# Second attention layer: three extra matmuls after each relative row while the pipeline fills

## The reference

```python
def _L1_attn_ref(x, Wq, Wk, Wv, Wo, E):        # 16 heads of 8, 4 key/value groups
    ...
    scores = jnp.einsum('bhqd,bhkd->bhqk', q, k)
    dist = jnp.clip(pos[None, :] - pos[:, None], -MAX_POS + 1, MAX_POS - 1) + MAX_POS - 1
    R = E[dist]
    bias = jnp.einsum('bhqd,kqd->bhqk', q, R)
    attn = jax.nn.softmax(scores + bias, axis=-1)
    out = jnp.einsum('bhqk,bhkd->bhqd', attn, v)
    ...
```

## Time and profile before

| | us |
|---|---|
| median of 3 runs (1812.39 to 1816.71) | 1813.37 |
| the profiled execution's own time | 1815.89 |
| its span, first to last instruction | 1814.2 |
| PE busy | 1449.7 (80%) |
| DVE busy | 1026.8 (57%) |
| ACT busy | 858.4 (47%) |
| POOL busy | 699.3 (39%) |

### The profile page before, as it was taken

How to read it: one execution, slowest core, us unless ns; L and a number is a source line. 1 busy time by engine, 2 the same in 40 slices (tenths; PEclk the granted TensorE clock), 3 DMA queues, 4 the chain that set the end, 5 groups by cost and what they waited for, 6 DMA issues and landing times. The chain is left out here.

```text
span 1814.2 us, 42125 instructions
## 1 busy us (share of the span) xinstructions
PE 1449.7 (80%) x15527; PEld 988.0 (54%) x15527; DVE 1026.8 (57%) x2775; ACT 858.4 (47%) x1544; POOL 699.3 (39%) x1372
## 2 busy tenths in 40 slices
PE   3799999869999993347992369999997699999935
PEld 2477777656776773225762235555555355555524
DVE  5666566475665655651332755656655566666453
ACT  2355455444555551001220237767764377777622
POOL 1266566425666660033553123433332233333300
PEclk9999999989999996568996668989987699999958
DMA  4000000000000000701442036767660467666400
GB/s 125 1 1 2 2 2 2 2 1 1 2 2 3 2 2 1 267 24 50 89 97 39 5 96 198 214 179 203 193 183 2 120 200 211 201 208 200 127 1 24
DMA packets 104953, 148.74 MB, mean 82 GB/s; under 512 B 13750, under 2 KB 61238, under 8 KB 104758
## 3 DMA queue, kind: packets, MB, share of 16 engines
q1 hardware_dynamic: 97974, 141.22, 26.4%
q0 software_dynamic: 6784, 4.87, 2.0%
HBM read 68.49 MB, written 77.21 MB: 80 GB/s over the span
## 5 line engine op out<-in xcount | busy, mean ns | idle before, releaser
L655 DVE CUSTOM_DVE_ANT_0 t_Z<-t_psS,a0b_L 128x1024 f32<-128x1024 f32 x256 | 310.1, 1220 | 151.9 <-issue 146.2
L713 ACT ACTIVATE t_Pt<-t_psT 128x512 f32<-128x512 f32 x512 | 278.8, 596 | 238.4 <-PE t_psT L612 238.4
L998 ACT ACTIVATE t_Pt<-t_psT 128x512 f32<-128x512 f32 x512 | 285.8, 595 | 144.7 <-PE t_psT L816 88.3
L901 DVE TENSOR_REDUCE t_mm<-t_psS 128x1 f32<-128x640 f32 (+1 forms) x256 | 219.5, 857 | 218.6 <-DMA t_A<-relative_rows 152.2
L612 PE MATMUL t_psT<-idf,t_Z 128*128 128x128 f32 x2048 | 282.6, 282 | 17.7 <-POOL t_Z L678 16.1
L678 POOL TENSOR_SCALAR t_Z<-t_Z,t_m 128x1024 f32<-128x1024 f32 x256 | 287.9, 1125 | 0.0
L612 PEld LDWEIGHTS t_psT<-idf,t_Z 128*128 128x128 f32 x2048 | 223.8, 143 | 105.8 <-ACT t_Pt L713 39.4
L802 PE MATMUL t_psS<-a1b_KT,a1b_QT 72*128 72x384 bf16 (+3 forms) x864 | 225.3, 314 | 12.2 <-DVE t_mm L902 11.9
L988 ACT ACTIVATE t_rows<-t_psT 128x512 f32<-128x512 f32 x256 | 153.1, 599 | 48.2 <-PE t_psT L794 41.2
L842 PE MATMUL t_psO<-t_Pt,t_Vh 128*32 128x128 f32 x4096 | 170.7, 286 | 1.9 <-DVE t_Os L925 1.6
L571 PE MATMUL t_psS<-a0b_KT,a0b_QT 72*128 72x512 bf16 (+1 forms) x512 | 155.4, 385 | 5.5 <-PEq L75 4.1
(11 more groups left out here) (260 smaller groups left out, 1820.2 us busy)
## 6 DMA issues: line engine op xcount, KB each, us to landing
relative_rows<-t_rows SPq DMA_DIRECT2D x256, 256.0 KB, 2.9
t_A<-relative_rows SPq DMA_DIRECT2D x192, 192.0 KB, 3.3
t_A<-relative_rows SPq DMA_DIRECT2D x64, 128.0 KB, 2.5
x_B<-in_b SPq DMA_DIRECT2D x1, 4096.0 KB, 18.5
x_A<-in_a SPq DMA_DIRECT2D x1, 4096.0 KB, 27.0
a1b_QT<-t_mr SPq DMA_DIRECT2D x192, 1.0 KB
expert_rows<-zp SPq DMA_DIRECT2D x1, 2740.0 KB, 12.7
x_xe<-expert_rows SPq DMA_DIRECT2D x8, 342.5 KB, 2.9
```

Of the source, the lines that this page charges most:

```text
L655: nc.vector.tensor_tensor_reduce(out=Z[:, j, :], in0=psS[:, j % 2, :], in1=L[:, qt, :], scale=1.0, scalar=3e38, op0=ALU.add, op1=ALU.min, ...
L713: nc.scalar.activation(Pt[:, qt % 2, j, half * (N // 2):(half + 1) * (N // 2)], psT[:, half, :], ACT.Exp).then_inc(s_exp, 1)
L901: v.reduce_max(mm[:, u % AR, 1:2], psS[:, u % 2, width:N], AX)
L998: nc.scalar.activation(Pt[:, q % PR, :], psT[:, unit_item(G, i) % RR, :], ACT.Exp).then_inc(s_exp, 1)
```

## The change

A function `keep_busy(n)` is added on TensorE, which issues n matmuls of the first keys by the first queries, 72 rows and 512 columns, into psO. It is called with n = 3 after every relative row of the turns -3, -2 and -1. It waits for nothing and signals nothing. Nobody reads what it writes: the first value sum of a group begins with `start=True`.

```diff
+                def keep_busy(n):
+
+                    for _ in range(n):
+                        nc.tensor.matmul(psO[:], QT[0:KR, 0, 0:P], KT[0:KR, 0, 0:512], start=True, stop=True)
+
                 def turn_max(G, out):
...
                         if i % 2:
                             if G + 3 < GROUPS:
                                 relative(G + 3, i // 2)
+                            if G < 0:
+                                keep_busy(3)
                             if i == 1 and G >= 1:
                                 values(G - 1, 6)
                                 values(G - 1, 7)
```

## The result

The changed kernel takes 1829.77 us as the median of 20 runs (1814.69 to 1841.44), the kernel before 1818.86 us in 20 runs taken beside them (1810.66 to 1832.21). The ratio is 1.0053 with a 95% interval of 1.003 to 1.0076: slower by 5.5 to 13.8 us, the way and about the size forecast (+7.4 us). The absolute time, forecast as 1820.8 us in a range of 1811.5 to 1828, lies outside. The profiled execution took 1823.52 us with a span of 1821.8 us, 7.6 us more than the span of before. Of all runs behind the ratios in this document one is left out as slow, a run of e11_rows128_one of 1868.18 us with a mean clock of 0.784.

The account below looks back on a forecast made before the run. The fill was taken as paced by bias transfers, with TensorE becoming the bound at clock 0.50. +3.9 us less 0.2 absorbed gave +3.7 per batch, +7.4 for both; on 1813.4 that is 1820.8 us, range 1811.5 to 1828.

Parts of the forecast that it names:

- The clock in the fill: In each batch's fill before turn 0, the added 72-row matmuls run at clock 0.50, but for the first 1.5 us.
- The price: In turns -2 and -1, three added matmuls cost 1.28 us at clock 0.50, making a tile's period 2.54 us, not 1.83.
- T0: Time from the first relative row to turn 0's first transpose: 26.2 us forecast, against 22.3 us before.
- 27.5 us at 0.50 throughout: TensorE's whole work in one fill if the clock were 0.50 all along: relative rows, added matmuls, scores and turned maxima.
- the 1.3 us for the start at full clock: Taken off the fill's 27.5 us because its first 1.5 us run at full clock, giving 26.2 us.
- The slack of 0.57 us: TensorE's free time per tile of turn -2 or -1: 1.26 us of work in a period of 1.83 us.
- Absorbed on the way: Table load and first waits in turn 0 hide some 0.2 us of the +3.9 us, leaving +3.7 us per batch.
- the last sign of the prediction: From first relative row to end of layer, time grows by 3 to 5 us per batch; otherwise the forecast is wrong.
- 3 us to either side: Widening of the forecast range for when the clock rises in turn 1, from earlier runs differing by 4.3 us.
- the base of the sum: Median of the earlier runs of the kernel before, 1813.4 us, to which +7.4 us was added for 1820.8 us.
- The rivals: Alternatives to the forecast; the first has the clock rise in the fill, saving up to 15.2 us in all, 12%.
- the rival: Clock rises in turn 0 rather than turn 1 in one batch, behind eight fp32 transposes, gaining about 6.5 us; 10%.

Follow-up runs that it names:

- e11_rows128_one: One added matmul of 128 rows (identity) after each relative row of the fill, in place of the change's three of 72 rows; ratio 1.0002 to the kernel before.
- e6_six_fillers: Six added matmuls of 72 rows after each relative row, in place of the change's three; one run, 1857.54 us.
- e1_rows128: The change with its three added matmuls reading 128 rows of the identity instead of 72 rows of keys and queries; ratio 0.9991 to the kernel before.
- e2_rows72_identity: The change with its three added matmuls reading 72 rows of the identity instead of keys and queries; ratio 1.0046 to the kernel before.
- e3_one_filler: The change with one added matmul of 72 rows after each relative row instead of three; ratio 0.9974 to the kernel before, 1.0008 when run again.
- e8_rows128_four: The change with four added matmuls of 128 rows (identity) instead of three of 72, none after the fill's last relative row; ratio 1.0034 to the kernel before.

## Why the prediction was right and where it was wrong

**The clock in the fill**: right, and shown. It was the decisive choice. The granted clock was 0.50 through 39.7 us of unbroken work in 72 rows (e6_six_fillers) and rose after 4.4 us with fillers of 128 rows (e1_rows128). The Trainium skill, page "TensorE: Matmul & The Clock Gate", section "What's actually happening", says that sustained matmul activity releases the throttle. For the fillers of 128 rows the trace agrees with it; for those of 72 rows it does not.

**The price**: right. Three fillers took 1.28 us, a tile 2.56 us against 2.54 predicted. T0 was predicted as 26.2 us and is 26.65, the delay 4.3 to 4.6 and not 3.9. The prediction's 27.5 us at 0.50 throughout is what the second batch of e2_rows72_identity shows, 27.6. The term that was mis-sized is the 1.3 us for the start at full clock: between the two batches of that run it is worth 0.85 us. The first two relative rows and six fillers took 2.44 us (1062.93 to 1065.37), where eight at 0.43 us would take 3.4. The slack of 0.57 us is that of turn -2; in turn -1 VectorE took a tile only every 2.2 us before, so there was more.

**Absorbed on the way**: the prediction took 0.2 us back and got +3.7 us per batch; measured by M1 it is 3.8 and 4.0 us. So some 0.6 us was absorbed, which makes up for the former error: the close agreement of the two sums, 7.7 us by turn 1 and 7.4 predicted, is partly luck. That the steady part hides none of it is consistent with the ratio's 5.5 to 13.8 us.

**To the end of the layer**: the last sign of the prediction, 3 to 5 us more per batch up to there, did not come. From the first relative row to the maxima turned in turn 30 it is 301.2 and 290.3 us before, 298.6 and 302.5 us with the change: 2.6 us less and 12.3 us more. What lies between is the clock after M1, at 0.50 for 27.3 us and none before, for 13.6 and 17.1 us now. As an estimate, with half of each low microsecond lost, these falls are worth -6.9 and +8.6 us. With the 3.8 and 4.0 us of M1 that makes -3.1 and +12.5 us, near the measured -2.6 and +12.3. So, by this estimate, the delay itself does reach the end, and the falls of the clock are larger than it.

**The absolute time**: wrong. The step that failed is the last in the change's part: "I add 3 us to either side for it, by the runs before, which differ by 4.3 us among themselves", together with the base of the sum, the median of those three runs. They gave 1813.37 us; 20 runs of the same kernel give a median of 1818.86 and a spread of 21.6 us, and the larger sets of runs beside the experiments have medians of 1824.85 (35 runs), 1818.75 (17) and 1816.13 us (29). So the base was 5.5 us too low, which by itself is more than the 3 us, and the falls of the clock move one batch by -6.9 or +8.6 us, by the estimate above. The measured median lies 9.0 us above the forecast: 5.5 us are the base, and 3.5 us are the difference of the medians, 10.9 us in place of 7.4. With the later base the same sum would have read 1826.3.

**The rivals**: the clock does not come up in the fill with these fillers. It can come up in turn 0: not in the change's profile, but in one batch of e2_rows72_identity and of e3_one_filler, in both behind the eight transposes, where the rival had placed it. The change does do what it says: it keeps TensorE busy. With these matmuls that did not raise the clock.

## What to carry to other kernels

Before filling idle time to hold the clock, look in the trace for what stood ahead of its rises and falls: here 72-row matmuls held TensorE busy for tens of microseconds at half clock, and fillers of all 128 rows raised it. Price a filler at the low clock and against the slack of the stage where it stands; here the twelve in the long first wait were free, and those beside the scores made the delay. And even the filler that raised the clock earned nothing that could be measured in the total; about 1.8 us of what it won in a batch by turn 1 was gone by turn 7, with longer waits for transfers: ask what an engine will wait for when its clock comes up early.

## What had not been expected

The executions of one and the same program differ by over 1%, and the granted clock goes with it: of the 20 runs of the change the fastest, 1814.69 us, had a mean clock of 0.894, and the slowest, 1841.44 us, one of 0.876. Falls of the clock in the steady part of the layer come and go from one execution to the next (after M1 none to 30.7 us at 0.50 per batch). A difference of half a per cent in one profiled execution says nothing here; distances inside a stage, as T0 and M1, repeat within 0.3 us where the clock takes the same course.

A clock at full speed is also lost easily. In e8_rows128_four it fell at the head of turn 0 after a stretch with 1.57 us of work in 3.40, and then stayed low for 13.6 us.
